# Masked attention scores kept in PSUM instead of a copy in SBUF (two-layer graph network, one core)

## The reference

```python
# layer 0
h = relu(layernorm(x))
A = adj @ h;  C = adj @ h + b
x = x + max_n relu(A[:, n] + (C - A))      # a max over the features
# layer 1, attention with 8 heads of 64
h = relu(layernorm(x))        # (x stands for the output of layer 0)
q, k, v = h @ Wq + bq, h @ Wk + bk, h @ Wv + bv
scores = q @ k^T / 8 + (adj == 0 ? -1e9 : 0)       # 8 x 128 x 128 per graph
x = x + softmax(scores) @ v
```

## Time and profile before

| | before |
|---|---|
| time, median of 3 runs | 1313.68 us |
| lowest and highest | 1312.29, 1314.34 us |
| the profiled execution's own time | 1313.61 us |
| its span in the trace | 1311.8 us |
| PE busy | 1289.5 us, 98% |
| DVE busy | 1058.9 us, 81% |
| ACT busy | 944.9 us, 72% |
| POOL busy | 1033.5 us, 79% |
| granted TensorE clock, mean | 0.996 |

### The profile page before, as it was taken

The page is one execution under the profiler, slowest core; times in us unless marked ns, Lnnn a source line. Parts: engine busy times, 40 slices in busy tenths (PEclk is TensorE's granted clock), DMA queues, the critical chain, the costliest instruction groups (busy, mean ns, idle before and its releaser), DMA issues.

```text
span 1311.8 us, 31156 instructions
## 1 busy us (share of the span) xinstructions
PE 1289.5 (98%) x11334; PEld 678.2 (52%) x11334; DVE 1058.9 (81%) x2207; ACT 944.9 (72%) x1461; POOL 1033.5 (79%) x1168
## 2 busy tenths in 40 slices
PE   7999999999999999999999999999999999999996
PEld 5455555555555555555555555555555555555554
DVE  7788888788788788788888888888887887887786
ACT  6877777777777777777777777777777777777555
POOL 5987877877877887887788788778778778778674
PEclk9999999999999999999999999999999999999998
DMA  5465655665565666556556655655555765764434
GB/s 195 84 139 125 139 135 130 131 137 136 122 145 137 122 137 137 130 131 143 130 124 145 136 122 144 139 121 138 135 131 132 138 135 124 143 137 114 101 79 113
DMA packets 434057, 171.72 MB, mean 131 GB/s; under 512 B 399337, under 2 KB 399474, under 8 KB 433906
## 3 DMA queue, kind: packets, MB, share of 16 engines
q1 hardware_dynamic: 433888, 169.72, 56.9%
q10 hardware_dynamic: 18, 0.00, 0.0%
HBM read 37.03 MB, written 33.55 MB: 54 GB/s over the span
## 4 chain that ended last, share of the span: by engine, by line
PE 92%; DVE 3%; ACT 2%; POOL 1%; issue 1%; DMA 0%; POOLq 0%; SPq 0%; ACTq 0%; DVEq 0%
PE proj L914 48%; PE proj L932 24%; PE proj L975 7%; PE sc L950 7%; PE proj L897 6%; DVE shifted L636 1%; DVE masked L624 0%; ACT h L439 0%; DVE row_max L628 0%; POOL h L327 0%; POOL inv_std L308 0%; POOL qkT L343 0%; ACT h L440 0%; DVE v L613 0%; DMA x_in<-in_x 0%
## 5 line engine op out<-in xcount | busy, mean ns | idle before, releaser
L914 PE MATMUL proj<-hT,w 128*128 128x512 f16 x3060 | 702.1, 379 | 0.6 <-ACT qk L453 0.6
L914 PEld LDWEIGHTS proj<-hT,w 128*128 128x128 f16 x3060 | 294.2, 98 | 353.3 <-ACT qk L453 1.1
L343 POOL TENSOR_TENSOR qkT<-qk,qkT 128x512 f16<-128x512 f32 x256 | 317.5, 1240 | 61.7 <-ACT qk L453 61.5
L932 PE MATMUL proj<-w,hT 128*128 128x512 f16 x1536 | 352.5, 379 | 2.6 <-DVE v L613 2.6
L350 POOL TENSOR_TENSOR probs<-probs 128x1024 f16<-128x1024 f32 x127 | 270.8, 2133 | 17.0 <-ACT probs L471 16.8
L469 ACT ACTIVATE probs<-shifted 128x1024 f16<-128x1024 f32 x127 | 134.2, 1057 | 180.4 <-DVE shifted L636 180.3
L451 ACT ACTIVATE qkT<-proj,bqk_up 128x512 f16<-128x512 f32 x256 | 173.4, 677 | 101.2 <-PE proj L914 97.5
L932 PEld LDWEIGHTS proj<-w,hT 128*128 128x128 f16 x1536 | 141.5, 98 | 154.5 <-DVE v L613 2.9
L613 DVE SCALAR_TENSOR_TENSOR v<-proj,v 128x512 f16<-128x512 f32 x128 | 88.4, 691 | 163.9 <-ACT v L459 163.9
L636 DVE TENSOR_TENSOR shifted<-masked,row_max 128x1024 f32<-128x1024 f32 x127 | 208.4, 1641 | 2.3
L658 DVE SCALAR_TENSOR_TENSOR y<-proj,out_scale,x 128x64 f32<-128x64 f32 x976 | 198.6, 277 | 4.3
(11 more groups left out here) (94 smaller groups left out, 1052.5 us busy)
## 6 DMA issues: line engine op xcount, KB each, us to landing
x_in<-in_x SPq DMA_DIRECT2D x128, 256.0 KB, 3.0
out_x<-y SPq DMA_DIRECT2D x128, 256.0 KB, 2.4
probsT<-probs SPq DMA_TRANSPOSE x127, 3.7
hT<-h SPq DMA_TRANSPOSE x124, 3.1
w_raw<-in_L_gnn_Wq SPq DMA_DIRECT2D x4, 256.0 KB, 5.4
w_raw<-in_L_gnn_Wk SPq DMA_DIRECT2D x1, 1024.0 KB, 7.9
w_raw<-in_L_gnn_Wv SPq DMA_DIRECT2D x1, 1024.0 KB, 11.0
bv_rows<-in_L_gnn_bv SPq DMA_DIRECT2D x1, 256.0 KB, 11.2
```

Source lines behind the costliest of these rows:

```text
L343: pool.tensor_tensor(qk_place(k, u, 1), qk32[:, u % 2, :], qk_place(k, u, 0), ALU.subtract).then_inc(qk_rest_done, 1)
L914: last = nc.tensor.matmul(proj[:, QK_BANKS[u % 2], :], w16[:, j, s, c, col * P:(col + 1) * P], hT[:, k // GROUP % HT_GROUPS, t, c, :, :].r ...
L932: last = nc.tensor.matmul(v_bank(m), hT[:, m // GROUP % HT_GROUPS, s, c, k % GROUP, :], w16[:, 2, t, c, :], start=(c == 0 and i == 0), sto ...
```

## The change

The SBUF tile `masked` is gone. `masked(m)` is now a view of the two PSUM banks of graph m: L624 reads the scores there and writes the masked scores over them, L628 and L636 read them there. L670, L674 and L677 do the same for the last graph. In exchange TensorE may write new scores into the banks only when the shift has read them: four waits name `shifted_done` where they named `masked_done`, with the same counts. No instruction is added or removed, and none changes its place in a queue.

```diff
-        masked = sb("masked", [P, H, P])
...
+        def masked(m):
+
+            return score_banks(m).rearrange("p t (h n) -> p (t h) n", n=P)
...
-                    nc.vector.scalar_tensor_tensor(masked[:, :, :], score_banks(m).rearrange("p t (h n) -> p (t h) n", n=P),
+                    nc.vector.scalar_tensor_tensor(masked(m), masked(m),
                                                    score_scale[:, :], mask8[:, :].unsqueeze(1).to_broadcast([P, H, P]),
                                                    ALU.mult, ALU.add).then_inc(masked_done, 1)
                     dve.wait_ge(masked_done, m + 1)
-                    nc.vector.tensor_reduce(row_max[:, :], masked[:, :, :], AX.X, ALU.max).then_inc(max_done, 1)
+                    nc.vector.tensor_reduce(row_max[:, :], masked(m), AX.X, ALU.max).then_inc(max_done, 1)
...
-                    nc.vector.tensor_tensor(shifted[:, :, :], masked[:, :, :],
+                    nc.vector.tensor_tensor(shifted[:, :, :], masked(m),
                                             row_max[:, :].unsqueeze(2).to_broadcast([P, H, P]), ALU.subtract).then_inc(shifted_done, 1)
...  (last_softmax: the same three edits, on masked(B - 1)[:, heads, :])
@@ scores(base, k)
-                    wait(pe, masked_done, m - 1)
+                    wait(pe, shifted_done, m - 1)
@@ probs_times_v(base, k)
                     elif m == B - 4:
-                        pe.wait_ge(masked_done, B - 1)
+                        pe.wait_ge(shifted_done, B - 1)
@@ last_probs_times_v(half)
-                pe.wait_ge(masked_done, B + half)
+                pe.wait_ge(shifted_done, B + half)
```

More of the change, by code:

```diff
@@ L669, in last_softmax @@
                 dve.wait_ge(s_ready, B)
-                nc.vector.scalar_tensor_tensor(masked[:, heads, :], score_banks(B - 1)[:, half, :].rearrange("p (h n) -> p h n", n=P),
+                nc.vector.scalar_tensor_tensor(masked(B - 1)[:, heads, :], masked(B - 1)[:, heads, :],
                                                score_scale[:, :], mask8[:, :].unsqueeze(1).to_broadcast([P, H // 2, P]),
@@ L673, in last_softmax @@
                 dve.wait_ge(masked_done, B + half)
-                nc.vector.tensor_reduce(row_max[:, heads], masked[:, heads, :], AX.X, ALU.max).then_inc(max_done, 1)
+                nc.vector.tensor_reduce(row_max[:, heads], masked(B - 1)[:, heads, :], AX.X, ALU.max).then_inc(max_done, 1)
                 dve.wait_ge(max_done, B + half)
                 dve.wait_ge(probs_done, B - 1)
-                nc.vector.tensor_tensor(shifted[:, heads, :], masked[:, heads, :],
+                nc.vector.tensor_tensor(shifted[:, heads, :], masked(B - 1)[:, heads, :],
                                         row_max[:, heads].unsqueeze(2).to_broadcast([P, H // 2, P]), ALU.subtract).then_inc(shifted_done, 1)
```

## The result

The changed kernel takes 1309.20 us, the median of eight runs (1308.58 to 1310.66), beside 1312.63 us for the kernel before (eight runs, 1312.29 to 1314.34). The ratio is 0.9971, 95% interval [0.9962, 0.9979]: 3.4 us less. Beside other experiments, on another chip, it took 1309.76 us against 1313.49, ratio 0.9974 [0.9964, 0.9984]. The forecast was 1310.2 us.

The account below looks back on a forecast made before the run. TensorE was taken to bound the kernel from 70 to 1261 us; 1313.61 less 0.95 at the start and 2.5 in the tail gave 1310.16, stated as 1310.2 us, with 1308.6 to 1313.9 for 8 in 10.

Parts of the forecast that it names:

- What bounds the kernel: Between 70 and 1261 us TensorE sets the pace, 19.85 us for two slots; VectorE's savings there bring nothing.
- The four waits: TensorE's waits passing from masked to shifted cost nothing: about 3.5 us slack in the steady part, other waits in the tail.
- The shift: VectorE's L636, reading PSUM and row_max, takes 1.24 us instead of up to 2.783, with nothing lost on GpSimd's side.
- the shift is held all the same: Rival: the shift, still a TENSOR_TENSOR with an SBUF operand, stays stretched; 1313.6 us; chance 12%.
- The row maximum: VectorE's maximum over 1024 numbers, now read from PSUM, takes at most 0.01 us more; the dearer end is 0.05.
- The masking: VectorE's masking, writing PSUM over what it reads, takes no longer; the ends are 0.05 us less and 1.28 more.
- The start: Slot 5, graph 0: GpSimd's L308 is no longer stretched, so TensorE's steady part begins 0.95 us earlier.
- The tail: Behind 1261 us: faster shifts of graphs 122, 123, 125 and 126 in VectorE's queue bring 2.5 us.
- The sum: Whole kernel, against the profiled execution: 1313.61 - 0.95 - 2.5 = 1310.16 us, stated as 1310.2, 0.27% less.
- slow writes: Rival: masking takes up to 2.56 us, hidden in the steady part, not in the tail; 1317.9 us; chance 10%.

Follow-up runs that it names:

- e3: The full change for graph 0 alone, all other graphs masked in SBUF as in the kernel before: 1311.79 us against 1312.92, ratio 0.9992.
- e4: The full change for graphs 122 to 127 alone, all others masked in SBUF as in the kernel before: 1310.15 us against 1312.92, ratio 0.9979.
- e1: The kernel before with only TensorE's four waits moved from masking to shift, still masked in SBUF: 1313.83 us against 1312.92, ratio 1.0007.
- e2: The kernel before with the four waits moved and the row maximum of graphs 0 to 126 in PSUM, scores in SBUF: 1309.51 us against 1312.92.
- e5: The changed kernel with each row maximum of graphs 8 to 119 computed once more, before the shift: 1342.34 us; kernel before 1313.57.
- e7: The changed kernel with VectorE's tail reordered, masking and maximum of graphs 124 and 126 moved ahead: 1307.77 us; kernel before 1313.57.
- e11: The changed kernel with the same tail order as e7, run again on another chip: 1309.09 us; kernel before 1313.49, ratio 0.9964.
- e6: The changed kernel with each row maximum of graphs 8 to 119 computed two more times: 1528.72 us; kernel before 1313.57, ratio 1.1639.

## Why the prediction was right

- **What bounds the kernel, and that most of VectorE's gain brings nothing**: right. 46 us of VectorE's busy time are gone and the steps are still 19.85 us. e3 and e4 show that the shifts of the 121 graphs between start and tail bring nothing.
- **The four waits at nothing**: right, by the marks in e1's trace. One reading on the way was off and changes nothing: the shift of 124 is done 0.9 us before VectorE begins graph 125, not over a microsecond.
- **The shift, from up to 2.78 to 1.24 us**: right in cause and nearly in size, 1.224. The cause was read from the rows beside each other; e2 shows it apart from the rest of the change. The rival that the shift is held all the same is out.
- **The row maximum, 0.01 us more**: 0.005. The Trainium skill's fixed cost of 120 cycles for a PSUM source against 58 ("VectorE: DVE Perf Modes", section "The TRN2 errata — SBUF-src ops pay a fixed extra latency per instruction") isn't borne out: 1.220 us from SBUF in the median before, 1.225 from PSUM now. The measurement decides.
- **The masking, no change**: 0.008 us more. Reading and writing the same banks in one instruction costs nothing that matters. The argument for it had a wrong figure: TensorE's 512 columns in 0.216 us are some three times VectorE's pace (1024 in 1.276), not five. No row had shown a VectorE write to PSUM, so this term was a guess with a reason.
- **The start, 0.95 us**: 0.91, and by the way that was named, one GpSimd instruction of 0.55 us held to 1.51, while the shift beside it stays as it is. e3 gives it alone.
- **The tail, 2.5 us**: 2.52, and inside it the scores of 124 by 1.20 (1.2 said) and `scaled_sum` of 123 by 1.82 (1.83 said). e4 gives it alone.
- **The sum**: 1310.16 was made against the profiled execution of before, which had met the lower clock in its last 20 us, and so lay 1.0 us above the median of eight runs, 1312.63. That is the miss of 1.0 us. The difference of 3.45 agrees with the marks, 3.43, to a few hundredths, and this is the mechanism; that the medians differ by just as much is luck, since the second pair of medians gives 3.7. The clock of this tail stands in none of the rows, and should: a tail that ends at a falling clock is no fair base for a sum of a few us.
- **Wrong: the price of slow writes.** The rival said that 2.56 us more of VectorE in a step would be hidden, "16.1 of 19.85, and 2 x 1.28 more still fits". e5 put 2.5 us in the same place and cost 33 us. By that, a slow write would have made a time near 1350 (an estimate), not 1317.9, and outside everything that was considered. The step that failed is taking cover from busy shares; the round over VectorE and ScalarE had 1.9 us to spare, by the estimate from e5, and before the change, with shifts of 1.40 and 1.89, about 1.0. It did not show because the writes are fast.

What stays open: why the clock falls in the tail in some executions and not in others, why the transposing DMA is slower in the kernels with the spare tile, and whether the 1.4 us of e7 and e11 are kept in the mean.

## What to carry to other kernels

Look in a trace for instructions of one line with a wide spread, and lay the other engines' rows beside the slow ones: where GpSimd's and VectorE's stretched rows interlock, moving even the smaller of two SBUF inputs to PSUM frees both. Ask of each that gets faster where it stands in a chain that the bound engine waits for; here at most four of 127 did, and one GpSimd instruction beside a fifth. And take an engine's slack from the round that its work goes through, with the other engines in it, not from its busy share: the same 1.2 us of work in each slot cost nothing behind the round and 33 us on it.

## What the runs showed of the hardware

- A VectorE TENSOR_TENSOR with both inputs in SBUF and a GpSimd instruction on SBUF don't overlap: the later one stands until the other ends. GpSimd's instruction of one number per partition took 1.51 us instead of 0.55 that way. With either of the two inputs in PSUM the same instruction, 1.22 us long, overlaps freely (e2: 1.208 to 1.221 in 127). That an operand of eight numbers, read over and over, counts as much as one of 1024 I had not known.
- VectorE writes PSUM as fast as SBUF, also over the banks that it reads: 1.284 against 1.276 us for 1024 numbers.
- In the steady part of e6 TensorE's granted clock fell in 34 steps of 55, behind a stand of TensorE of 2.1 us, and twelve products took up to 4.44 us instead of 2.75. Other steps with the same stand kept the clock at 1.00, so the rows give no rule.
- TensorE's granted clock in the last 20 us differs from execution to execution of one kernel (0.76 or 1.00 in the same stretch of the changed kernel), after a tail in which TensorE has stood for 1.5 and 2.5 us, and makes some 1.6 us of the time.
